# Search a step later, candidates and fold moved, four groups of sums behind the second convolution

## The reference

```python
n = ln_c(x)                                  # over the channels, each pixel
g = groupnorm(n, 8 groups) * gn_w + gn_b     # over pixels and 8 channels
x = x + n + w2 @ relu(w1 @ g + b1) + b2      # two 1x1 convolutions

t = to_tokens(x)                             # 16384 tokens of 64
u = ln_t(t)
probs = softmax(u @ gate_w.T + gate_b, over the tokens)      # 32 experts
vals, idx = top_k(probs of each expert, 8)
pooled = einsum('bked,bke->bed', u[idx], vals)
out = gelu([pooled, 1] @ weight1) -> [., 1] @ weight2        # each expert
t = t + scatter_add(idx, out * vals)
```

## Time and profile before

| what | us |
|---|---|
| median of 3 runs | 639.11 |
| lowest and highest run | 637.30, 641.03 |
| profiled execution, its own time | 639.6 |
| its span in the profile | 637.9 |
| PE busy in the span | 535.4 (84%) |
| DVE busy | 487.2 (76%) |
| ACT busy | 435.3 (68%) |

### The profile page before, as it was taken

One profiled execution on the slowest core, in us unless ns is written; L12 is line 12 of the kernel. 1 busy time (PEld: TensorE's weight loads), 2 busy tenths in 40 slices (PEclk: granted clock), 3 DMA queues, 4 the chain that ended last, 5 costly groups with the idle time before them and its releaser, 6 DMA issues.

```text
span 637.9 us, 14170 instructions
## 1 busy us (share of the span) xinstructions
PE 535.4 (84%) x5732; PEld 270.3 (42%) x5732; DVE 487.2 (76%) x950; ACT 435.3 (68%) x651; POOL 189.6 (30%) x116
## 2 busy tenths in 40 slices
PE   2749999898998899889989899989887988876982
PEld 1324444444444344444444444444443433434762
DVE  5574556689888988898789878988888687799620
ACT  2463779677976797679767976797677855984110
POOL 1007435023502260217020802080207145121144
PEclk9955999999999999999999999999998998987595
DMA  8960144714471447244634454445401255430000
GB/s 195 195 144 0 68 133 142 188 68 133 133 199 67 134 133 191 76 133 134 168 98 134 115 160 123 133 101 165 133 35 67 76 182 154 146 100 5 6 15 19
DMA packets 26752, 73.38 MB, mean 115 GB/s; under 512 B 4152, under 2 KB 4152, under 8 KB 22592
## 3 DMA queue, kind: packets, MB, share of 16 engines
q1 hardware_dynamic: 25664, 71.44, 40.9%
q0 software_dynamic: 1024, 1.05, 0.6%
HBM read 38.40 MB, written 34.08 MB: 114 GB/s over the span
## 4 chain that ended last, share of the span: by engine, by line
PE 41%; DVE 30%; ACT 13%; issue 12%; DMA 2%; POOL 1%; SPq 0%; ACTq 0%; DVEq 0%; POOLq 0%
PE st L372 11%; ACT junk L801 7%; DVE xs L948 7%; PE cv L383 6%; PE cv L391 6%; PE tl L400 6%; PE bc L494 5%; DVE us L938 5%; DVE lg L936 3%; DVE top_i L1035 2%; ACT tok L766 2%; DVE us L940 2%; DVE cnd L1030 2%; DMA xs<-in_x 2%; PE tl L409 2%
## 5 line engine op out<-in xcount | busy, mean ns | idle before, releaser
L1426 POOL TENSOR_TENSOR xs<-xs,us 128x1024 f32<-128x1024 f32 x64 | 151.2, 2379 | 367.2 <-DVE xs L948 173.4
L948 DVE SCALAR_TENSOR_TENSOR xs<-cv,vecs,xs 128x1024 f32<-128x1024 f32 x64 | 82.1, 1282 | 47.8 <-PE cv L391 47.7
L794 ACT ACTIVATE sqc<-us 128x1024 f32<-128x1024 f32 x64 | 67.5, 1054 | 46.2 <-DVE us L938 45.4
L761 ACT ACTIVATE hid<-cv,b1n 128x1024 f32<-128x1024 f32 x64 | 71.2, 1113 | 36.5 <-PE cv L383 36.0
L938 DVE TENSOR_TENSOR us<-xs,bc 128x1024 f32<-128x1024 f32 x60 | 73.0, 1216 | 19.7 <-PE bc L494 19.3
L400 PEld LDWEIGHTS tl<-ident,xs 128*128 128x128 f32 x512 | 63.8, 195 | 53.9 <-issue 53.9
L372 PE MATMUL st<-xs,stat_w 128*32 128x256 f32 x1024 | 74.5, 413 | 10.5 <-DMA xs<-in_x 9.4
L801 ACT ACTIVATE junk<-us 128x1024 bf16<-128x1024 f32 x64 | 67.3, 1051 | 22.8 <-DVE gsum L940 22.1
L940 DVE CUSTOM_DVE_ANT_0 us<-us,bc 128x1024 f32<-128x1024 f32 x60 | 72.9, 1215 | 11.2 <-PE bc L494 9.9
L400 PE MATMUL tl<-ident,xs 128*128 128x128 f32 x512 | 76.4, 294 | 0.9 <-ACT lg L776 0.9
L409 PE MATMUL tl<-xs,gcen 128*32 128x256 f32 x1024 | 69.4, 389 | 8.0 <-ACT tok L766 7.9
(11 more groups left out here) (210 smaller groups left out, 652.4 us busy)
## 6 DMA issues: line engine op xcount, KB each, us to landing
xs<-in_x SPq DMA_DIRECT2D x64, 512.0 KB, 7.0
out_rows<-tok SPq DMA_DIRECT2D x64, 512.0 KB
us<-in_e_w SPq DMA_DIRECT2D x8, 260.0 KB
xs<-in_e_w SPq DMA_DIRECT2D x8, 256.0 KB
sqc<-out_rows,idx_all POOLq DMA_INDIRECT x16
out_rows<-sqc,idx_all POOLq DMA_INDIRECT x16, 2.1
vecs<-in_b SPq DMA_DIRECT2D x4, 0.2 KB, 14.0
gate_bias<-in_gate_b SPq DMA_DIRECT2D x4, 0.1 KB, 12.3
```

What stands on the lines that cost most here:

```text
L948: nc.vector.scalar_tensor_tensor(out=xu, in0=cv[:], scalar=vecs[:, 3:4], in1=xu, op0=ALU.add, op1=ALU.add).then_inc(x1_done, 1)
L1426: nc.gpsimd.tensor_tensor(xu, xu, su, ALU.add).then_inc(s_done, 1)
```

## The change

- **The search of places and values 2 and 3 comes a step later** in all iterations but the last: `top_values` in steps 1, 2, 4 and 5, `top_places` in 2, 3, 5 and 6, `explog` in 3, 4, 6 and 7. The last iteration keeps the old tables (second entry, chosen by `not p1`).
- **Candidates** move from the end of step 6 to step 7, in front of x1 and behind `norm_weights`.
- **The fold** moves from place (7, 0), in front of conv2 of step 7, to (7, 1), behind it; on DVE its two copies move behind x1 and `norm_bias`. In iteration 7 it stays at (7, 1).
- **Four groups of sums** move: the squares' fourth group (step 0) and second group (step 5) behind conv2 and the spread (s, 1), in front of the logits; `x1_sums` of step 6 likewise; `x1_sums` of step 2 behind the logits. This holds in all iterations.

No instruction is added or removed.

```diff
-M_JOB, LAST_M_JOB = (7, 0), (7, 1)
+M_JOB, TAIL_M_JOB = (7, 1), (7, 0)
...
-VALUES_AT = {1: 0, 2: 1, 3: 2, 4: 3}
-PLACES_AT = {2: 0, 3: 1, 4: 2, 5: 3}
-EXPLOG_AT = {3: 0, 4: 1, 5: 2, 6: 3}
+VALUES_AT = ({1: 0, 2: 1, 4: 2, 5: 3}, {1: 0, 2: 1, 3: 2, 4: 3})
+PLACES_AT = ({2: 0, 3: 1, 5: 2, 6: 3}, {2: 0, 3: 1, 4: 2, 5: 3})
+EXPLOG_AT = ({3: 0, 4: 1, 6: 2, 7: 3}, {3: 0, 4: 1, 5: 2, 6: 3})
...
-        jobs[LAST_M_JOB if it == NB - 1 else M_JOB] = ("M", it - 1)
+        jobs[M_JOB if it < NB else TAIL_M_JOB] = ("M", it - 1)
...
                 if s == 0 and b >= 0:
                     x1_sums(b, b % 2, NG - 1)
-                    x1_square_sums(b, NG - 1)
...
-                if s in (2, 4, 6):
-                    x1_sums(it, par, s // 2 - 1)
-                if s in (3, 5, 7):
+                if s == 4:
+                    x1_sums(it, par, 1)
+                if s in (3, 7):
                     x1_square_sums(it, (s - 3) // 2)
...
                     spread_at(it, (s, 1))
+                if s == 0 and b >= 0:
+                    x1_square_sums(b, NG - 1)
+                if s == 5:
+                    x1_square_sums(it, 1)
+                if s == 6:
+                    x1_sums(it, par, 2)
                 if b >= 0:
                     logits(b, b % 2, u)
+                if s == 2:
+                    x1_sums(it, par, 0)
...
+                if s == NU - 1 and t >= 0 and p1:
+                    candidates(t)
                 x1(it, par, s)
...
-                if s == 6 and t >= 0:
+                if s == 6 and t >= 0 and not p1:
                     candidates(t)
```

More of the change, by code:

```diff
@@ L845, in step @@
                     square_at(it, (s - 1, 2))
-                if t >= 0 and s in EXPLOG_AT:
-                    explog(t, EXPLOG_AT[s])
+                if t >= 0 and s in EXPLOG_AT[not p1]:
+                    explog(t, EXPLOG_AT[not p1][s])
                 if s == 6 and not p1:
@@ L1135, in step @@
                     ln2_rstd(NB - 1)
-                if t >= 0 and s in PLACES_AT:
-                    top_places(t, PLACES_AT[s])
+                if t >= 0 and s in PLACES_AT[not p1]:
+                    top_places(t, PLACES_AT[not p1][s])
                 use_at(it, (s, 2))
@@ L1142, in step @@
                     rstd(n)
-                if t >= 0 and s in VALUES_AT:
-                    top_values(t, VALUES_AT[s])
+                if t >= 0 and s in VALUES_AT[not p1]:
+                    top_values(t, VALUES_AT[not p1][s])
                 if s == 5 and not p1:
                     ln2_variance(NB - 1)
-                if s == 6 and t >= 0:
+                if s == 6 and t >= 0 and not p1:
                     candidates(t)
```

## The result

The changed kernel is slower: 650.5 us in the median of 4 runs (647.72 to 652.23) against 638.81 before, a ratio of 1.0176 with a 95% interval of 1.0143 to 1.0209. 647.1 was forecast, so the sign and the range (640.5 to 652.5) held, and the loss, 11.7 us, is larger than the 8.0 of the sum. The profiled execution took 650.84, its span is 649.1 against 637.9.

What follows compares the result with a forecast made beforehand. No engine was full; a better order could win at most 6.7 us per 65.20 us period. Terms +4.9, +6.0, -0.7, -1.5, -0.7 gave +8.0 on 639.6, so 647.6; median 0.5 lower, 647.1 us, range 640.5 to 652.5.

Steps and rivals of the forecast that it cites:

- Steps 0 to 4: Image's first steps: step 0 net 0, x1 of step 2 0.88 us earlier, step 4 another 0.57, together 1.45.
- Steps 5 and 6: Stretch up to norm_rsqrt: ACT has no gap to close, so norm_rsqrt and norm_weights come only 0.95 us earlier.
- Step 7: From norm_weights to next conv1: 3.20 us through candidates and fold, 1.77 later; net 0.82 an iteration, +4.9 over six.
- The clock: PE idles 2.8 us before the fold in iterations 1 to 6; four falls to half clock behind it, +6.0 us.
- the fall of iteration 6: Existing half clock behind step 4's wait in iteration 6: may go as that wait shortens, half of 1.4 us, -0.7.
- Iterations 0 and 7: First and last iterations, gaining from the moved sums: -1.5 us for iteration 0, -0.7 for iteration 7.
- No fall of the clock: Rival at the fold's wait: PE stalls but stays at 2.4 GHz, 641.1 to 641.8 us; no or one fall, 0.17.
- Other matmuls don't pass the waiting fold: Denies the rival in step 7 that other matmuls pass the fold and x1 sets conv1: 637.7 us, chance 0.04.
- ACT does hold the gain: Denies the rival that norm_rsqrt starts over 1.8 us earlier and norm_weights ends 2.2 earlier: 634.5 us, chance 0.10.
- the gains did arrive: Denies the rival that the 0.88 and 0.57 us of steps 2 to 4 are lost elsewhere: 654.7 us, chance 0.09.

Runs made afterwards that it cites:

- the filled kernels: Extra matmuls in step 4's waits: on the changed kernel with candidates in front of norm_weights, 627.21 us; on the kernel before with only the sums moved, 628.3 us.

## Why the prediction was right, and where it was short

**Steps 0 to 4.** Iteration 5 of the changed kernel starts at full clock, at 379.10, so it can be compared with the old schedule. Its x1 of step 2 and its first multiplication of step 4:

```profile
401.49 1.28 DVE L956 SCALAR_TENSOR_TENSOR xs<-cv,vecs,xs 128x1024 f32<-128x1024 f32 x1 [0.34 <-PE cv L392]
417.69 1.22 DVE L948 CUSTOM_DVE_ANT_0 us<-us,bc 128x1024 f32<-128x1024 f32 x1 [0.60 <-PE bc L495]
```

x1 comes 22.39 us behind the first conv1, before 23.10: 0.71 earlier, 0.88 was forecast. The multiplication starts 38.59 behind it in place of 39.88: 1.29 earlier, 1.45 was forecast. Both fall short by about 0.16 us, and most of that is there at x1 of step 1 already (14.72 behind conv1 against 14.58). The forecast had put step 0, with the fold's copies in it, at a net of nothing, and took 0.2 us off for them only in steps 5 and 6.

**Steps 5 and 6.** ACT holds the gain. From relu of step 5 to the end of norm_rsqrt in iteration 4 of the changed kernel (ACT's busy time is the fourth, 17.61):

```profile
356.66:374.71 18.05, 16.34 (x182) 8.32 (x182) 15.11 (x30) 17.61 (x29) 10.15 (x5) 1.00 0.41 118
```

It is busy for 17.61 of 18.05 us. The stretch is 0.5 us longer than before; 0.41 of that is one new wait, for PE behind the sums of step 5, where 0.3 was forecast. The last instruction of norm_weights comes 0.78 us earlier in iteration 5 (62.79 behind conv1, before 63.57), 0.95 was forecast. The kernel with the sums of steps 5 and 6 alone shows by itself that ACT holds the gain. One reading was lucky: the forecast took 0.88 from the sums and 0.57 from the later search, and, as the filled kernels show, the sums alone bring the whole gain at norm_rsqrt.

**Step 7.** 3.20 us were forecast from norm_weights to the next conv1. At the end of iteration 4, where the clock does not fall, the candidates start at 375.85 and conv1 at 379.10: 3.25. The forecast wait for the fold was 2.8 us, 2.87 was measured. The net length, forecast as 0.82 an iteration, is 1.0 in the kernel with the filled wait. Over iterations 1 to 6 the stall is 5.6 us there, once the new fall in step 4 of iteration 5 (1.6 us) is taken off; 4.9 was forecast. This term was right, a little low.

**The clock.** This is the step that was mis-sized: +6.0 for four falls at the turns and -0.7 for the fall of iteration 6, +5.3 together. Iterations 1 to 6 are 15.4 us longer in the profile; less the 5.6 of the stall some 9.8 are left, and filling the wait took 8 to 10. Two parts of it were off. At the turns there were five falls in place of four. From the last instruction of norm_weights to the next conv1 it is 3.45 us in iteration 4, which has none, and 4.52, 3.77, 4.39, 4.85 and 4.67 in iterations 1, 2, 3, 5 and 6. Behind the turn norm_rsqrt is 61.40 us behind conv1 in iteration 5, and by falls at the turn 2.3 later in iteration 3 and under 0.3 later in the others. Together that is 7.6 us: the short ones cost 1.2 to 1.5 each, about as priced, the long one of iterations 2 to 3 cost 2.7. And the fall of iteration 6 did not go but grew: norm_rsqrt of iteration 6 was 1.9 us later than in a steady iteration before, and is 3.9 later now, +2.0 in place of -0.7. Two stretches with such falls:

```profile
240.00:250.00 10.00, 9.21 (x64) 4.39 (x64) 6.27 (x20) 5.10 (x7) 0.00 (x0) 0.66 0.60 157
486.00:500.00 14.00, 11.84 (x93) 5.48 (x82) 10.23 (x15) 8.93 (x14) 10.24 (x5) 0.63 0.19 72
```

A mean clock of 0.66 over 10 us is half clock for 6.8 of them, 0.63 over 14 us half clock for 10.4. The second is the fall of iteration 6:

```profile
489.33 0.79 PE L495 MATMUL bc<-rstd_s,spread 32*128 32x256 f32 x4 [1.83 <-DVE gsum L948]
490.05 1.98 PE L384 MATMUL cv<-us,w1n 64*64 64x512 f32 x8
491.96 1.97 PE L401 MATMUL tl<-ident,xs 128*128 128x128 f32 x8
493.87 0.79 PE L495 MATMUL bc<-rstd_s,spread 32*128 32x256 f32 x4
494.59 1.98 PE L392 MATMUL cv<-hid,w2bd 64*64 64x512 f32 x8
```

Up to conv2 all is at half clock, where in the kernel before only conv1 and the transposes were the earlier trace rows. I had priced every fall like the two read in the earlier trace rows. The trace of the kernel before had a long one too, in its last iteration, behind a wait of 3.97 us:

```profile
567.00:580.00 13.00, 10.16 (x100) 6.59 (x104) 12.52 (x28) 6.46 (x13) 1.95 (x2) 0.61 0.14 47
```

That is half clock for some 10 us. Why some falls last two or three times as long stays open. The argument from idle times of 1.1 to 1.2 us, which had brought no fall, also judged waits one by one; the experiments had falls behind 0.32 and 0.82 us.

**Iterations 0 and 7.** -1.5 was forecast for iteration 0, -1.95 measured; for iteration 7 and the end -0.7, measured -1.1. The start, untouched, is 1.2 shorter. That these agree is in part luck. In the other profiles with the same four groups of sums moved, iteration 0 takes 58.4 to 60.5 us, by the falls that it happens to have. Outside iterations 1 to 6 the span is 4.3 us shorter where 2.2 was forecast, which hides a part of what the clock cost.

**The rivals.** No fall of the clock is refuted for this kernel. Where the fold's wait is filled the time is 640.3 us; 641.1 to 641.8 were worked out for no fall. Other matmuls don't pass the waiting fold: the logits start right behind it in every iteration, 0.62 or 0.63 us where it runs at full clock, and norm_bias, whose weights were done at 375.74, waits until 378.78 in iteration 4. The Trainium skill (TensorE: Matmul & The Clock Gate, "Architectural detail: the array is 16× 32×32, not 1× 128×128") gives TensorE a reorder window that can pull weight loads ahead of matmuls; in these rows no matmul passed another. ACT does hold the gain: norm_rsqrt starts 0.8 us earlier, not 1.8. And the gains did arrive, 0.78 of 0.95 us.

## What to carry to other kernels

Where an instruction with a wait is moved, list what stands behind it in its engine's order and on whose path that lies: here three short things behind one fold, which itself nobody was in a hurry for. Look also for an idle time of the engine just in front of the new place, as the 1.64 us here. A gain inside a stretch in which another engine has no gap is worth nothing until that engine's list is changed, so find its last idle moment first. And price waits of PE twice, once as time and once as what they do to its clock: the second was the larger here, and was bought back by useless matmuls in the wait.

## What the runs showed of the hardware

Half clock does not need one long wait. Waits of 0.33 and 0.83 us in one step were followed by it in iterations 2 and 4 of the kernel with the candidates in the gap, but not in its iterations 3 and 5, and in none of iterations 2 to 5 of the one with norm_rsqrt moved, which has the same waits. Iteration 6 of that kernel has one of 1.83 us, also without a fall. The kernel before has even longer ones at that place and no fall in iterations 2 to 5; here in iteration 4:

```profile
349.47 0.50 PE L494 MATMUL bc<-rstd_s,spread 32*128 32x256 f32 x4 [0.90 <-DVE gsum L940]
351.80 0.50 PE L494 MATMUL bc<-rstd_s,spread 32*128 32x256 f32 x4 [0.83 <-DVE gsum L940]
```

Waits of 2.86 to 3.17 us brought it in five of six iterations at one place and not in the sixth. So a wait makes a fall possible, and what decides the single case is not shown. A short fall, over some four groups of matmuls as at the turn to iteration 4, cost 1.2 to 1.5 us, and half clock could also last for 7 or 10 us. Filling 0.6 us of a wait of 0.8, or 2.0 of 2.87, removed the falls behind that wait in the profiled runs; one in iteration 6 began in front of the filled wait, behind 0.36 and 0.90 us.
